# A quarter of the routing table, the row numbers and the experts' numbers made inside the first turn of the loop

## The reference, cut to what matters

```python
def reference(x, ...):                       # x: (4, 1024, 256), 4096 tokens
    xn = _layernorm(x)
    return x + _attn(xn, ...) + _ffn(xn, ...)

def _attn(x, ...):                           # RWKV-6, 4 heads of 64
    x_last = x shifted by one token; b_a = x_last - x
    h   = tanh((x + b_a * miu_x) @ A).reshape(5, B * T, 32)
    miu = einsum('smk,skc->smc', h, Bp).reshape(5, B, T, C) + lam
    x5  = x + b_a * miu                      # five mixtures: w, k, v, r, g
    w = td_miu + tanh(w_in @ tdA) @ tdB
    k = k_in @ Wk.T * exp(minimum(w, 0));  v = v_in @ Wv.T;  r = r_in @ Wr.T
    g = tanh(g_in @ Wg1) @ Wg2
    y = wkv6(r, k, v, w, u)                  # a recurrence over the tokens
    return (groupnorm(y) * gamma + beta) * g @ Wo.T

def _ffn(x, Wr, br, W1, b1, W2, b2):         # 8 experts, one per token
    probs  = softmax(tokens @ Wr + br);  expert = argmax(probs)
    h      = relu(tokens @ W1[expert] + b1[expert])
    return (h @ W2[expert] + b2[expert]) * max_prob
```

## Time and profile before

| | us |
|---|---|
| median of 3 runs | 570.43 (569.09, 570.43, 576.64) |
| the profiled execution | 570.0 |
| its span, first to last instruction | 568.7 |
| TensorE busy | 523.6 (92% of the span) |
| VectorE busy | 440.8 (78%) |
| ScalarE busy | 334.8 (59%) |
| GpSimd busy | 195.1 (34%) |
| mean granted TensorE clock | 0.985 of full |

### The profile page before, as it was taken

The page is one execution under the profiler, slowest core; times in us unless marked ns, Lnnn a source line. Parts: engine busy times, 40 slices in busy tenths (PEclk is TensorE's granted clock), DMA queues, the critical chain, the costliest instruction groups (busy, mean ns, idle before and its releaser), DMA issues. The chain is left out here.

```text
span 568.7 us, 20264 instructions
## 1 busy us (share of the span) xinstructions
PE 523.6 (92%) x7946; PEld 463.5 (82%) x7946; DVE 440.8 (78%) x1104; ACT 334.8 (59%) x756; POOL 195.1 (34%) x156
## 2 busy tenths in 40 slices
PE   2889797988799999999999999999999999999984
PEld 2568686877698899989899888999997999988873
DVE  6877899999558686868869796969676887879552
ACT  4964656126374656666575657575655656575751
POOL 7901010123233443523425242443442433523332
PEclk9999999799799999999999999999999999999998
DMA  8979662789533443433342525153443334332324
GB/s 286 298 279 283 175 169 62 173 294 303 131 86 55 96 71 86 80 85 62 78 80 47 111 37 105 37 110 56 93 73 85 63 83 72 63 50 47 50 44 47
DMA packets 57632, 64.03 MB, mean 113 GB/s; under 512 B 10705, under 2 KB 51922, under 8 KB 57394
## 3 DMA queue, kind: packets, MB, share of 16 engines
q1 hardware_dynamic: 44722, 47.90, 30.2%
q0 software_dynamic: 11840, 14.42, 17.4%
q10 hardware_dynamic: 976, 0.41, 0.3%
HBM read 42.92 MB, written 24.12 MB: 118 GB/s over the span
## 5 line engine op out<-in xcount | busy, mean ns | idle before, releaser
L1796 POOL DMA_INDIRECT out<-rows,dst_row x39 | 63.8, 1635 | 213.1 <-DVE rows L1193 181.2
L713 PE MATMUL F<-w,hsT 128*128 x312 | 76.8, 390 | 3.7 <-DMA w<-in_W 3.2
L705 PE MATMUL F<-xsT,w1s 128*128 128x128 f32 x624 | 76.9, 276 | 2.1 <-ACT xsT L1573 1.1
L1065 DVE SCALAR_TENSOR_TENSOR mix<-G,vec,ba 128x256 f32<-128x256 f32 x160 | 69.6, 476 | 11.9 <-PE G L475 11.8
L705 PEld LDWEIGHTS F<-xsT,w1s 128*128 128x128 f32 x624 | 74.6, 192 | 4.7 <-issue 1.7
L713 PEld LDWEIGHTS F<-w,hsT 128*128 128x128 f32 x312 | 58.3, 193 | 12.5 <-issue 4.1
L1591 ACT ACTIVATE hsT<-F,b1c 128x128 f32<-128x128 f32 x156 | 44.7, 369 | 35.0 <-PE F L705 35.0
L1104 DVE COPY_PREDICATED AP_<-msk,LL 128x256 f32<-128x256 uint32 x96 | 51.0, 532 | 15.9 <-issue 10.6
L1126 DVE TENSOR_TENSOR RK<-RK,D 128x256 f32<-128x256 f32 x112 | 47.3, 422 | 17.4 <-issue 10.4
L1073 DVE TENSOR_TENSOR mix<-mix,xnT 128x512 f32<-128x512 f32 x80 | 55.1, 688 | 1.6
L1782 POOL DMA_INDIRECT rows<-xn_d,src_row x39 | 40.8, 1047 | 30.4 <-PE F L694 12.9
(11 more groups left out here) (192 smaller groups left out, 1187.6 us busy)
## 6 DMA issues: line engine op xcount, KB each, us to landing
cd<-cd_d SPq DMA_DIRECT2D x30, 320.0 KB, 5.9
w<-in_W SPq DMA_DIRECT2D x16, 512.0 KB, 9.2
cd_d<-w SPq DMA_DIRECT2D x32, 160.0 KB, 2.7
b2t<-in_b SPq DMA_DIRECT2D x39, 128.0 KB, 3.3
w<-in_x SPq DMA_DIRECT2D x8, 512.0 KB, 8.9
xn_d<-w SPq DMA_DIRECT2D x8, 512.0 KB
out<-in_x SPq DMA_DIRECT2D x8, 512.0 KB, 5.5
out<-res POOLq DMA_DIRECT2D x16, 256.0 KB, 4.9
```

What stands on the lines that cost most here:

```text
L705: i1 = pe.matmul(FB[:, k * P:(k + 1) * P], w1s[:, cc, k, :], xsT[:, cc, :], start=(cc == 0), stop=(cc == 1))
L713: i1 = pe.matmul(FB[:, 0:C], hsT[:, k, :], w2[:, bass.ds(number[f] * (HC * C) + k * C, C)], start=(k == 0), stop=(k == HC - 1))
L1065: i1 = dve.scalar_tensor_tensor(mixed_in(u, c, n, cc), bk[:, cc * UN:(cc + 1) * UN], cvec(LAM + CC * n, cc), ba[:, cc, :, :].rearrange("p ...
L1796: pool.indirect_dma_start(io["out"], bass.IndirectOffsetOnAxis(dst_row[:, f:f + 1], 0), ys[:, f % 2, :], None, compute_op=ALU.add).then_in ...
```

## The change

Four things change. On TensorE `table(3)` leaves the prologue for the loop's first turn, behind `mixed(1, 1, 1)`, and each group of the table now raises the semaphore `inv`. On VectorE `at_rows(2)` goes ahead of `grow(1, 0, 8)`, and `at_rows(3)`, the experts' numbers, the copy of the table and the row numbers go into the first turn. SyncE asks for W2 as 7, 0, 1, ... 6: piece 7 waits for nothing, pieces 0 to 3 for the table's group that lies in their place, 4 to 6 follow piece 3. The bias of tile 0 is asked for by ScalarE in the first turn, ahead of `weights(0)`.

```diff
             def table(g):
                 ...
-                if g == 3:
-                    i1.then_inc(s["inv"])
+                i1.then_inc(s["inv"])
             # TensorE, half(h)
                     mixed(u, c + 1, 1)
+                    if h == 1:
+                        table(3)
                     decay_down(u, c + 1)
             # TensorE, prologue
             receptance(0, 1)
-            table(3)
             gated_back(0, 0)
             # VectorE
             def table():
-                dve.wait_ge(s["inv"], 1)
+                dve.wait_ge(s["inv"], 4)
             # VectorE, half(h)
                 gate_terms(*v)
+                if h == 1:
+                    at_rows(3)
                 mixed(u, c + 1, 1)
                 added(u, c + 1, 1)
+                if h == 1:
+                    experts_of_tiles()
+                    table()
+                    rows_of_tiles()
             # VectorE, prologue
+            at_rows(2)
             grow(1, 0, 8)
             mixed(0, 1, 3)
-            at_rows(2)
-            at_rows(3)
             ...
             grow(1, 0, 32)
-            experts_of_tiles()
-            table()
-            rows_of_tiles()
             grow(1, 0, 64)
             # ScalarE
+            def first_bias():
+                act.wait_ge(s["ex"], 1)
+                e = act.value_load(expert[0:1, 0:1], min_val=0, max_val=E - 1)
+                act.dma_start(b2t[:, 0, :], io["b2"][...]...).then_inc(s["b20"], 16)
                 if h == 1:
+                    first_bias()
                     weights(0)
             # SyncE
             def bias(f):
                 if f > 1:
                     sp.wait_ge(s["fy"], f - 1)
+                elif f == 1:
+                    sp.wait_ge(s["ex"], 1)
-            sp.wait_ge(s["ex"], 1)
-            bias(0)
-            sp.wait_ge(s["inv"], 1)
-            for e in range(E):
+            for e in (7, 0, 1, 2, 3, 4, 5, 6):
+                if e < 4:
+                    sp.wait_ge(s["inv"], e + 1)
                 sp.dma_start(w2[:, e * HC * C:(e + 1) * HC * C]...).then_inc(s["ew2"], 16)
```

More of the change, by code:

```diff
@@ L1565, in last_bias @@
                 act.activation(b2t[:, f % 2, :], b2t[:, f % 2, :], ACT.Copy, scale=of_row[:, f, 1:2]).then_inc(s["bp"])
+            def first_bias():
+                act.wait_ge(s["ex"], 1)
+                e = act.value_load(expert[0:1, 0:1], min_val=0, max_val=E - 1)
+                act.dma_start(b2t[:, 0, :], io["b2"][bass.ds(e * C, C)].partition_broadcast(P)).then_inc(s["b20"], 16)
             number = {}
```

## The result

| | before | with the change |
|---|---|---|
| median of 22 runs each | 573.9 us | 576.66 us |
| lowest and highest | 569.09 to 580.21 | 573.29 to 582.56 |
| ratio, 95% interval | | 1.006 [1.0034, 1.0086] |
| profiled execution, its span | 570.0, 568.7 us | 580.88, 579.6 us |
| TensorE busy, granted clock | 523.6 us, 0.985 | 528.2 us, 0.982 |

The change costs 0.6%, that is 3.4 us of 573.9, with 2.0 and 4.9 us as the ends of the interval. The ratio leaves out the slowest few runs of each kernel, which the medians take in; the text goes by the ratio. The forecast was 2.7 us less than before.

What follows compares the result with a forecast made beforehand. TensorE's own work was taken to bound the kernel behind the first turn. +1.1 - 3.24 - 2.5 gave -4.6; the late bias made VectorE decide, at -2.7 against 570.0: 567.3 us, range 564.3 to 571.3.

Steps and rivals of the forecast that it cites:

- its credit of 5.7 us: At down(0): the W2 wait of 3.24 us goes, and 2.5 us of slow clock behind it.
- the first new wait: First turn, ahead of table(3): TensorE waits 2.3 us for VectorE's at_rows(3).
- The first gather: First turn: rows land at 136.9 to 138.9, TensorE asks at 137.8; cost 0 to 1.1 us, taken as 0.
- the second chain: First turn: late bias holds ScalarE's saved level 4, grow 4 waits 2.4 us, TensorE at middle_levels about 1.3 us.
- the start of `last_levels`: End of the prologue: 1.9 us earlier, at 122.4 instead of 124.31.
- The prologue: VectorE's at_rows(3) leaves, 1.17 us; at_rows(2) moves into idle time ahead of grow 8, 1.01 us; 1.9 taken.
- The rival: The clock falls at the new wait ahead of table(3), costing 3.4 us: 570.7 us; chance 0.3.
- The bias: First turn, ScalarE's last_bias(0): lands 4.5 us from issue, at 143.0, with 2.9 and 7.0 as the ends.
- the 0.6 by which VectorE was last in the forecast: At the fourth last_levels: VectorE is ready at 153.1, TensorE's own way gives 152.5, so VectorE decides.
- The double fall: A second clock fall at middle_levels behind 1.3 us idle: up to 573 us; left out of the range.
- two rivals: Clock falls ahead of table(3): 570.7 us, chance 0.3; bias lands in 7 us or more: 569.8, chance 0.08.
- Both profiles alike with a fixed shift behind 160 us: Sign to check: behind the fourth last_levels the profiles differ only by a constant shift.

Runs made afterwards that it cites:

- w2_half: The kernel before with only the first 256 of 512 rows of each expert's W2 loaded (wrong expert outputs): ratio 0.991.
- both_early: The changed kernel with at_rows(3) back in the prologue ahead of grow 64 and the first bias asked for right behind decay_down: ratio 0.9953.
- w2_alone: The kernel before with W2 asked for piece by piece as in the change, the first bias still SyncE's behind W2: ratio 0.9996.
- w2_bias: The kernel before with W2 asked for piece by piece and the first bias asked for by ScalarE at the head of the first turn: ratio 0.9911.
- bias_early: The changed kernel with the first bias asked for by ScalarE right behind decay_down: ratio 1.0012.
- moves_alone: The changed kernel with W2 asked for in one go behind the whole table, as before: ratio 1.0124.
- before_again: The kernel before, unaltered, profiled once more: 44.45 us from value(0, 1) to the second gated_back.
- after_again: The changed kernel, unaltered, profiled once more: 50.61 us from value(0, 1) to the second gated_back.
- rows_early: The changed kernel with at_rows(3) put back into the prologue, ahead of grow 64: ratio 1.002.
- all_early_2: Second run of the changed kernel with at_rows(3) and experts' numbers ahead of grow 64, table(3) ahead of output, row numbers behind gate_terms, bias at turn's head: ratio 0.9922.

## Why the prediction was wrong

**What held.** W2: no wait at `down(0)`, and its credit of 5.7 us lies near w2_half's 5.1. The place and size of the first new wait: 2.3 us forecast, 2.39 measured, put down to VectorE. The first gather cost nothing, though only because TensorE came 2.9 us later than forecast: in both_early it took 8.7 us from issue to use, over the 5.0 to 7.0 that the forecast had. The shape of the second chain (ScalarE at `last_bias(0)`, `grow` 4, `middle_levels`) is as described.

**What hit by luck** is the start of `last_levels`, forecast at 122.4 and measured at 122.05. Of those 2.26 us against before, 1.55 had come about by `value(0, 1)`: the fall of the clock behind the wait of 2.74 us near 100 was over by 105 in the changed kernel's profile, and lasted to 110 in before's (0.67 from 105 to 110). From `value(0, 1)` on, the prologue gave 0.7 us in both profiles of the change (`gated_back` at 7.5 for 8.2; w2_alone and w2_bias, with the prologue of before, have 8.5, so 1.0 at most), where 1.9 were forecast.

**What failed** is above all the choice of the likeliest case: that TensorE's clock would stand through the 2.3 us ahead of `table(3)`, and that the bias would land in 4.5 us. By the rows, in order:

- *The prologue.* The forecast put `at_rows(2)` into 1.01 us of idle time of VectorE ahead of `grow` 8. TensorE came sooner in the changed kernel, and VectorE has no such idle time there: `grow` 8 (L1126 at 111.28) stands right behind `at_rows(2)`, 0.44 us behind the start of `value(0, 1)`, where before it was 0.99 ahead of it. This term was 1.2 us too large.
- *The clock at `table(3)`.* It fell, in both profiles with the change, in bias_early (0.66 from 130 to 135) and in moves_alone (the same). From the table's start to `decay_down` it took 3.4 us for 1.8, and from there to the first `tokens` 8.86 us where it was 7.24 (131.83 to 140.69, against 129.42 to 136.66): 1.6 + 1.6 = 3.2 us. The rival had priced this at 3.4 and had a chance of 0.3. The comparison of waits that stood for the chance ("2.74 fell, 1.63 didn't") was of two single waits in one execution. before_again shows that it was no rule: behind the same waits of 0.78 and 1.64 us the clock fell there too. In the changed kernel the wait of 2.39 us came behind two others, of 1.34 and 1.64 us, with 4 us of work between.
- *The bias.* From issue to landing it took 5.7 us in moves_alone and 6.0 in after_again, and in the change 5.8 from issue to use (141.08 to 146.86), against 4.5. VectorE so waited 3.36 us for 2.4, TensorE 2.61 for 1.3: 1.3 us. That is within the bounds of 2.9 and 7.0, above the 4.5 that was taken. The Trainium skill, "DMA: Bandwidth & Descriptors", "Queues, rings and completion order", says that the engines go round the queues that have work; the prediction drew a quick landing from it, and the runs disagree with that. Not standing in SyncE's queue did not make the landing quick. From 140 to 145 us the DMA engines were busy throughout, by a share of 1.08 in the changed kernel's windows, at 265 GB/s.
- *The clock at `middle_levels`.* Behind the wait there came a second fall, in both profiles with the change: from it to `down(0)` it took 3.31 us where w2_bias needs 1.91, and from `down(0)` to the fourth `last_levels` 7.29 us (152.44 to 159.73) for w2_bias's 5.65 (144.74 to 150.39). That is 3.0 us, and takes back the 2.5 that the vanished wait for W2 had given in clock.

The sum is 1.2 + 3.2 + 1.3 + 3.0 = 8.7 us, less the 0.6 by which VectorE was last in the forecast: 8.1. From the start of `value(0, 1)` the fourth `last_levels` was forecast at 153.1 - 112.39 = 40.7 us and came at 159.73 - 110.84 = 48.9, 8.2 us later (49.1 in after_again). Against before's 43.4 that is 5.5 us late instead of 2.7 early. The runs agree on the sign, but their 3.4 us [2.0, 4.9] are less than that, for which no cause is shown.

**The range.** The double fall stood in the first rival, as "up to 573", that is 3.0 us over the profiled execution; the ratio gives 3.4. So the mechanism that came was written down, with its price, and then left out of the range: two rivals were treated as alternatives with small chances each. They stand on one chain, and a late bias lengthens the wait behind which the clock can fall a second time. It did so in both profiles of the change; behind rows_early's 1.86 us at the same place it didn't, and behind moves_alone's 2.58 us only with the third wait. Together they should have had more than the "some 0.15" that was left out.

**The base.** 573.9 was the median of before in 22 runs, 570.43 in the three shown; 3.5 us of the miss of 9.4 are this; the rest is in the steps above. The profiled execution was a favourable one: before_again came to `value(0, 1)` 3.0 us later, by the same instructions, and its turn of the loop about 375 us took 33.0 us instead of 30.8. TensorE's waits there, behind 165 us, in the second profile of before:

```profile
PE G L538 <- issue: 1.9, 1, 1.9
PE F L705 <- issue: 1.7, 2, 1.4
```

In the first profile no wait of this kind is over 0.6 us. "Both profiles alike with a fixed shift behind 160 us" so failed as a test, and two executions of one kernel fail it as well.

## What to carry to other kernels

Before moving a step behind the engine that bounds the kernel, look at who stands idle a few microseconds earlier: a new wait next to old ones can be charged twice, once as idle time and once as work at the lower clock, here 2.4 and 3.2 us. A small transfer that someone waits for is asked for as early as its address is known, by an engine whose queue isn't held: W2's early pieces gave nothing measurable with the bias behind them on SyncE, and 0.9% with it on ScalarE, 6 us earlier. Read a gain or a loss between two marks around the edit, since a hit in time from the span's start can be another stretch's luck. And don't count on an engine's idle time that another engine's slow clock had made. Where two rivals stand on one chain, price them together, and give the sum a chance of its own.

## What the runs showed of the hardware

- **The clock doesn't go by the length of one wait.** With waits of 0.78, 1.64 and 1.13 us it stayed at 1.00 in w2_bias and in the first profile of before, and fell to 0.75 in before_again behind the first two of them. In both_early it fell (0.80 and 0.85 from 120 to 130) with nothing over 1.64 us. Behind the wait of 2.4 us ahead of `table(3)` it fell in all four profiles that had one, for 6.8 us in the two of the change and for 3.4 in bias_early and moves_alone ((1 - 0.66) x 5 x 2). But moves_alone's 2.58 us ahead of `middle_levels` left it at 1.00 until 151, and so did both_early's 2.19 ahead of `tokens` from 140 to 150, while it fell at w2_alone's 2.21 ahead of `decay_down`. One trace without a fall is no promise.
- **TensorE's waits for "issue".** A stop of 1.5 to 1.9 us without any releaser stands at one and the same place of the program, between 370 and 382 us, in eight of the thirteen profiles, but not in the first of before or in after_again. Behind it the clock was 0.66 in three (1.46 us in w2_alone, 1.61 in w2_bias, 1.87 in all_early_2) and 1.00 in five (1.88 in before_again, 1.53 in the change). In w2_alone:

```profile
374.74 0.27 PE L537 MATMUL G<-mix,wg 128*32 128x64 f32 x2 [1.46 <-issue]
```

  That turn of the loop took 34.4 us there, for 30.8 in the first profile of before, so such stops are a part of what makes the rest of the span differ between executions. What causes them was not tried.
- **An issuing queue is a resource.** Eight pieces of W2 held SyncE for 10.0 us before, which is 1.3 us each. Asked for early they held it for 15.85 us in w2_alone and 18.31 in the change; 2.7 and 7.3 us of that were waits for the table, so 13.2 and 11.0 us are left. The Trainium skill, "DMA: Bandwidth & Descriptors", "Issuing engines are not separate DMA queues", says that another issuing engine saves only the issue time, usually small beside the transfer. For one piece this agrees: 1.3 us beside a landing of 9.2 (median of W1's and W2's in the profile of before). The bias in w2_alone stood behind all eight.
- **Asking for a DMA costs ScalarE more than its row says.** The row of the DMA has 0.37 us, but the copy behind it stood 1.26 us for "issue" in the change, where before there was no such wait. The loads of the expert's number into a register, ahead of the DMA and behind it, are part of this.
